# Attention and expert layer on one core: one layer norm a sequence ahead, a regrouped value product, and the differences to the maximum on GpSimd

## What is computed

```python
x = x + layernorm(attn(layernorm(x)))     # x: (16, 512, 128)
x = x + layernorm(ffn(layernorm(x)))
# attn: scores = einsum(Qh, Kh) + einsum(Qh, rel_k_table[clip(k - q, -2, 2) + 2]);  scores /= sqrt(8)
#       p = softmax(where(causal, scores, -1e9))
#       out = einsum(p, Vh) + einsum(p, rel_v_table[idx]);  return out @ W_o + b_o
# ffn:  shared silu(x @ sw1) * (x @ sw3) @ sw2, plus the two best of 8 gelu experts by sigmoid gates
```

## Time and profile before

| | us |
|---|---|
| median of 3 runs | 1033.69 (1032.93 to 1034.54) |
| profiled execution, its own time | 1030.79 |
| its span, first to last instruction | 1029.1 |
| attention, up to the last exponential | about 722 |
| a step with all four stages | about 41.5 |

### The profile page before, as it was taken

How to read it: one execution, slowest core, us unless ns; L and a number is a source line. 1 busy time by engine, 2 the same in 40 slices (tenths; PEclk the granted TensorE clock), 3 DMA queues, 4 the chain that set the end, 5 groups by cost and what they waited for, 6 DMA issues and landing times. The chain is left out here.

```text
span 1029.1 us, 25739 instructions
## 1 busy us (share of the span) xinstructions
PE 898.8 (87%) x8935; PEld 526.4 (51%) x8935; DVE 817.6 (79%) x1948; ACT 680.5 (66%) x1315; POOL 728.0 (71%) x946
## 2 busy tenths in 40 slices
PE   2888988999899988998999898887679999999995
PEld 0443444544445444444444444433357777777773
...
DMA packets 58828, 70.88 MB, mean 69 GB/s; under 512 B 8944, under 2 KB 34416, under 8 KB 58720
## 3 DMA queue, kind: packets, MB, share of 16 engines
...
q10 hardware_dynamic: 2288, 0.42, 0.2%
...
## 5 line engine op out<-in xcount | busy, mean ns | idle before, releaser
L1137 DVE TENSOR_REDUCE mx<-ps_s 128x1 f32<-128x512 f32 (+2 forms) x640 | 410.2, 682 | 75.2 <-PE ps_s L1549 74.2
L809 ACT ACTIVATE prob<-ps_e 128x512 f32<-128x512 f32 x640 | 352.0, 608 | 110.3 <-PE ps_e L1506 110.2
L651 POOL TENSOR_SCALAR_AFFINE_SELECT prob<-prob 128x516 f32<-128x516 f32 (+1 forms) x320 | 176.6, 576 | 150.2 <-ACT prob L809 150.1
L1530 PE MATMUL ps_s<-ks,qs 31*128 31x512 f16 (+3 forms) x1024 | 196.5, 324 | 32.2 <-DVE mx L1137 27.0
L1572 PE MATMUL ps_av<-prob,vp 128*32 128x512 f32 (+3 forms) x2048 | 202.5, 495 | 4.3 <-POOL prob L651 4.2
L731 POOL TENSOR_TENSOR hidden_low<-hidden,hidden_high 128x512 fp32r<-128x512 f32 x144 | 191.0, 1354 | 12.0 <-ACT hidden_high L998 10.7
L1506 PE MATMUL ps_e<-qs,ks 32*128 32x512 f16 (+3 forms) x1024 | 167.9, 316 | 6.2 <-ACT prob L809 2.0
L1530 PEld LDWEIGHTS ps_s<-ks,qs 31*128 31x128 f16 x1024 | 54.9, 94 | 167.6 <-issue 89.4
L1549 PE MATMUL ps_s<-masked_at,below 32*128 32x64 bf16 (+3 forms) x2560 | 135.0, 192 | 0.0
L998 ACT CAST hidden_high<-hidden 128x512 fp32r<-128x512 f32 x160 | 98.0, 613 | 30.7 <-DVE hidden L1450 27.5
L1549 PEld LDWEIGHTS ps_s<-masked_at,below 32*128 32x128 bf16 x2560 | 105.6, 98 | 20.0 <-issue 4.1
...
## 6 DMA issues: line engine op xcount, KB each, us to landing
gate_rows<-gates_dram SPq DMA_DIRECT2D x128, 256.0 KB, 3.7
...
```

What stands on the lines that cost most here:

```text
L651: pool.affine_select(out=v, in_=v, compare_op=ALU.is_ge, fill=0.0, base=-2, pattern=cols, channel_multiplier=-1).then_inc(S["p_masked"], 1)
L809: act.activation(prob[g % 2][:, u, b, :], ps_e[bank][:, :], ACT.Exp, scale=SCALE).then_inc(S["e_done"], 1)
L1137: dve.tensor_reduce(out, src, AX.X, ALU.max).then_inc(s_free[bank], 1)
L1530: pe.matmul(scores[:, at:at + P * (qt + 1)], qs[par][rows, pr, P * qt:P * qt + P], ks[par][rows, pr, 0:P * (qt + 1)], start=(n == 0), stop ...
```

## The change

Four things are changed at once, and the places of the side work on every engine with them.

1. **First norm one sequence ahead.** Norm1 of sequence t0+1 is made in step t0 (DVE's statistics and POOL's `normalise`), so that xT moves from round 6 to round 0. q moves from round 9 to 3 and k from 10 to 5. `xnT` has two buffers, since xT now writes the next sequence's before v0, moved from round 5 to 8, has read the one before. Sequence 2 is loaded by itself.
2. **Output projection in round 9** instead of 11; oT stays in 7. s_tok moves from 7 to 10.
3. **Value banks shared by two groups.** `vp` puts an odd group's columns 16 further than an even group's, and both groups add into one bank. So ACT copies, PE transposes and DVE reads two results (av0, av1) per sequence instead of four, each twice as wide; the values are copied on ACT in two halves.
4. **Differences on POOL.** The two DVE instructions for d in each `max_half` become one POOL instruction.

```diff
+AT = {"xT": 0, "e_sums": 1, "q": 3, "m1": 4, "k": 5, "av1": 6, "oT": 7, "v0": 8, "oproj": 9, "s_tok": 10,
+      "m0": 15, "av0": 17, "xn2": 18, "logits": 19}
...
-        vp = [sb(f"vp{i}", [P, NT, H, 32]) for i in range(2)]
+        vp = [sb(f"vp{i}", [P, NT * NGRP, 4, 2 * WIDE]) for i in range(2)]
...
+            def differences(st, s, half):
+
+                pool.wait_ge(S["m16_ready"], st.at(2 * s + half + 1, 2))
+                hs = slice(half * 8, half * 8 + 8)
+                pool.tensor_tensor(d01[:, :, :, hs], s_tok[:, :, :, hs],
+                                   m16[:, :, hs].unsqueeze(1).to_broadcast([P, 2, NT, 8]),
+                                   ALU.subtract).then_inc(S["d_ready"], 1)
...
                 if st.B:
+                    differences(st, st.b, 1)
                     near_half(st, st.b, 1)
-                masks(0, 3)
-                if st.F:
-                    normalise(st, st.f, xn[:, :, :], tiles(xr[:, st.seq(st.f), :]), mv1, var1, rs1,
-                              "stats1").then_inc(S["xn_ready"], 1)
-                masks(3, 10)
+                masks(0, 5)
                 if st.F:
                     split(st)
+                    if st.f + 1 < NSEQ:
+                        norm1(st.f + 1)
                 if st.t0 == 0:
                     masked_columns()
...
-                act.copy(vp[st.a % 2][:, :, :, 0:D].rearrange("p t h d -> p (t h) d"),
-                         ps_s[bank][:, :].rearrange("p (c d) -> p c d", d=D)).then_inc(S["v_ready"], 1)
+                of = ps_s[bank][:, :].rearrange("p (c j d) -> p c j d", j=4, d=D)
+                for q in range(2):
+                    last = act.copy(vp[st.a % 2][:, q::2, :, WIDE * q:WIDE * q + D], of[:, q::2])
+                last.then_inc(S["v_ready"], 1)
...
-            def av_out(st, s, g):
-
-                act.wait_ge(S["av_full"], st.at(NGRP * s + g + 1, NGRP))
-                act.copy(av_s[g % 2][:, :], ps_av[:, :]).then_inc(S["av_copied"], 1)
+            def av_out(st, s, part):
+
+                act.wait_ge(S["av_full"], st.at(NGRP * s + 2 * part + 2, NGRP))
+                act.copy(av_s[part][:, :], ps_av[:, :]).then_inc(S["av_copied"], 1)
...
+                need(dve, S["d_ready"], st.at(2 * st.a, 2))
...
-                for k in range(2):
-                    last = dve.scalar_tensor_tensor(d01[:, k, :, hs], m16[:, :, hs], -1.0, s_tok[:, k, :, hs],
-                                                    ALU.mult, ALU.add)
...
-                own.mark(dve.tensor_tensor(den[:, :, hs], v[:, :, :, D], p_near[par][:, :, 4 * g:4 * g + 4], ALU.add))
-                cols = slice(4 * g * D, 4 * g * D + 4 * D)
-                dve.tensor_tensor(num[:, :, hs, :], v[:, :, :, 0:D], near[par][:, :, cols].rearrange(
-                    "p t (j d) -> p t j d", d=D), ALU.add).then_inc(S["misc_free"], 1)
-                if g % 2 == 0:
-                    return
+                own.mark(dve.tensor_tensor(den[:, :, :, :], v[:, :, :, :, D], p_near[par][:, :, both].rearrange(
+                    "p t (q j) -> p q t j", q=2), ALU.add))
+                dve.tensor_tensor(num[:, :, :, :, :], v[:, :, :, :, 0:D], near[par][:, :, cols].rearrange(
+                    "p t (q j d) -> p q t j d", q=2, d=D), ALU.add).then_inc(S["misc_free"], 1)
...
+                after = st.t0 + 1 if 0 < st.t0 < NSEQ - 1 else None
...
-                if kt == 0:
-
-                    need(pe, S["av_copied"], st.at(NGRP * s + g, NGRP))
+                if kt == 0 and g % 2 == 0:
+
+                    need(pe, S["av_copied"], st.at(NPART * s + g // 2, NPART))
...
-                    last = pe.matmul(ps_av[32 * j:32 * j + 32, P * kt:SEQ], vp[par][:, kt, 4 * g + j, :],
+                    last = pe.matmul(ps_av[32 * j:32 * j + 32, P * kt:SEQ], vp[par][:, NGRP * kt + g, j, :],
                                      prob[g % 2][:, u, j % 2, at:at + w],
-                                     start=(kt == 0), stop=(kt == NT - 1))
+                                     start=(kt == 0 and g % 2 == 0), stop=(kt == NT - 1 and g % 2 == 1))
```

More of the change, by code:

```diff
@@ L208, in end @@
     def end(self):
-        if LOOP0 <= self.st.t0 < NSEQ and self.per_step != self.n - self.first:
+        if LOOP0 <= self.st.t0 < NSEQ - 1 and self.per_step != self.n - self.first:
             raise AssertionError((self.n - self.first, self.per_step))
@@ L322, in block_kernel @@
         av_s = [sb(f"av_s{i}", [P, SEQ]) for i in range(2)]
-        den = sb("den", [P, NT, 8])
-        rden = sb("rden", [P, NT, 8])
-        num = sb("num", [P, NT, 8, D])
+        den = sb("den", [P, 2, NT, 4])
+        rden = sb("rden", [P, 2, NT, 4])
+        num = sb("num", [P, 2, NT, 4, D])
         o_tok = sb("o_tok", [P, NT, P])
@@ L404, in block_kernel @@
         S = {n: sem(n) for n in names}
-        x_loaded = [S["x_loaded0"], S["x_loaded1"], S["x_loaded2"]]
+        x_loaded = [S[f"x_loaded{i}"] for i in range(4)]
         stacks = [[S[f"stacks{par}{half}"] for half in range(2)] for par in range(2)]
@@ L714, in step @@
                     selectors()
-                masks(12, 15)
+                masks(10, 14)
+                if st.A:
+                    differences(st, st.a, 0)
+                masks(14, 15)
                 if st.t0 == NSEQ + 2:
@@ L816, in xT_out @@
                 act.wait_ge(S["e_full"], n + 1)
-                act.copy(xnT[:, 1:1 + SEQ], ps_e[bank][:, :]).then_inc(S["e_done"], 1)
+                act.copy(xnT[st.f % 2][:, 1:1 + SEQ], ps_e[bank][:, :]).then_inc(S["e_done"], 1)
             def q_out(st):
@@ L1191, in av_tok_out @@
                 own.settle()
-                own.mark(dve.reciprocal(rden[:, :, :], den[:, :, :]))
+                own.mark(dve.reciprocal(rden[:, :, :, :], den[:, :, :, :]))
                 own.settle()
-                dve.wait_ge(S["misc_free"], st.misc(f"av{g}") + 1)
-                both = slice(4 * (g - 1) * D, 4 * (g + 1) * D)
-                dve.tensor_tensor(o_tok[:, :, both].rearrange("p t (j d) -> p t j d", d=D), num[:, :, :, :],
-                                  rden[:, :, :].unsqueeze(3).to_broadcast([P, NT, 8, D]),
+                dve.wait_ge(S["misc_free"], st.misc(f"av{part}") + 1)
@@ L1199, in av_tok_out @@
+                dve.tensor_tensor(o_tok[:, :, cols].rearrange("p t (q j d) -> p q t j d", q=2, d=D), num[:, :, :, :, :],
+                                  rden[:, :, :, :].unsqueeze(4).to_broadcast([P, 2, NT, 4, D]),
                                   ALU.mult).then_inc(S["o_ready"], 1)
@@ L1330, in step @@
                     gates_second(0, EARLY)
[L1331 removed]
+                maxima(13, 16)
                 if st.A:
[L1333 to L1334 removed]
+                    values_out(st)
+                maxima(16, 18)
                 if st.C:
```

195 lines of the change are left out of this document (94 added, 101 removed).

## The result

The changed kernel takes 1056.63 us in the median (1055.06 to 1068.95, 4 runs) against 1033.62: a ratio of 1.025, 95% interval 1.017 to 1.033. It is slower by 23 us where 1025 was forecast, 9 faster; that it is slower is beyond doubt, that it is so by over 2% is not. The profiled execution took 1058.02, its span is 1056.3, 27 above the profiled execution before.

A forecast was written before the change was run, and what follows sets the result against it. PE and its waits bound rounds 17 to 7 (-0.45), DVE rounds 8 to 16 (-0.2); with gaps and clock -0.6 a step, -8 over 13 steps, -8.7 with the ends: 1025, forecast 1016 to 1031 (0.42), whole range 1000 to 1046.

The forecast's parts named there:

- the term for q and k in rounds 8 to 16: Front of DVE's stretch: q and k, 2.24 us of PE, kept DVE short of score units; their leaving gains 2.2 a step.
- Rounds 17 to 7: Stretch over the turn of the step, paced by PE and what it waits for: forecast -0.45 us a step.
- out: v0, 1.16: Rounds 17 to 7: moving v0 to round 8 takes 1.16 us of PE work out of this stretch.
- Rounds 8 to 16: Stretch in which DVE sets the pace, with PE behind the s ring: forecast -0.2 us a step.
- PE pays for that once more: Projection, one round after v0: it needs the bank v_near empties; DVE being slower, the wait costs PE, not the end.
- ACT: Four copies between its sixth and tenth exponential, 1.7 us net; mostly covered by idle time, so +0.4 a step.
- Differences: d of the second half on POOL, 0.35 us, makes exponential p<-d about 1 us later: +0.4 a step, between 0 and 1.0.
- The clock: PE's lower 1.2 GHz level, which comes behind waits: its cost falls from 1.4 to 1.0 us a step.
- A: Rival, chance 0.24: ACT's copies and v0's bank outlast the gains, waits bring the low clock, +0.9 a step: 1044.
- D: Rival, chance 0.04: POOL's SBUF reads hold DVE back, o_tok's median over 700 ns, 1.9 us a step: 1050.
- C: Rival, chance 0.12: no change; DVE's work and waits set the step, its savings go into idling at v0: 1034.
- B: Rival, chance 0.18: without the waits for xr and xn the clock stays up, step 39.0: 1001.

The follow-up runs named there:

- e9: The changed kernel with q back in round 9 and k in round 10, their copies where they were before: 1018.5 us.
- h6: The e9 kernel with five idle products of a constant on PE ahead of round 3, without q's copies: 1023.1 us.
- e6: The changed kernel with v0 in round 9 and the output projection in round 11: 1037.5 us.
- e4: The changed kernel with eight idle products of a constant on PE ahead of the output projection in each step: 1039.7 us.
- h3: The changed kernel with k alone back in round 10, q left in round 3: 1065.6 us.
- h1: The e9 kernel with the differences to the maximum (d) back on DVE: 1019.2 us.

## Why the prediction was wrong

The step that failed first is the term for q and k in rounds 8 to 16, forecast as a gain of 2.2 a step: there they had cost nothing, and without q there PE stands before v0's bank and loses the clock. With q alone back in round 9 (h5) the kernel takes 1019.6 instead of 1056.6. The terms one by one:

**What bounds the kernel: wrong in its half.** "From round 17 to round 7 PE sets the pace" was read off a trace in which PE waits for xn in that stretch. Without that wait DVE is nearly always busy in rounds 2 to 6, too (idle 0.4 in e9). PE work placed there has no cover: 1.2 us of it in round 3 cost 0.65 a step (h6).

**Rounds 17 to 7, forecast -0.45 a step.** Measured: 23.6 against 23.1, so +0.5. The wait for xn did go, 1.3. The step that failed here is "out: v0, 1.16". v0 stands ahead of round 8, at the end of the same stretch, and left nothing; e6, which moves it on to round 9, has rounds 0 to 7 1.2 shorter. q and k cost what was said, 2.24.

**Rounds 8 to 16, forecast -0.2.** Measured: 20.5 against 18.3, so +2.2. The wait for v0 was sized right (1.8), in part by luck: the product ahead of v0 is not one of 1.07 in round 8 but that of round 7, 1.28. Two steps failed. "PE pays for that once more ... this wait costs PE and not the end": it was 1.7 us of stand, right before the low clock, and e4 shows 17 to 20 us in it. And "q and k, 2.24 of PE, ... are gone: I take -2.2": this was the largest term and had the wrong sign. In rounds 9 and 10 they were free and kept PE at work: rounds 8 to 10 take 6.5 us with both of them (e9) and with q alone (h5). q's place is worth 37 us (h5 against the changed kernel) or 47 (e9 against h3). That the trace shows no wait there was read as room to gain, when it was the cover that hid them.

**ACT**, 0.4 with bounds 0 to 1.7: the size is not parted from the clock, 9 to 15 us in all. **Differences**: 0.31 us on POOL (0.35 forecast), p<-d waits 9.3 us in ten times, 0.9 each (1 forecast), but of the +0.4 on the path nothing was found: with d on DVE the step is 0.3 longer (h1). **num**: 0.414 for one of two widths against 2 x 0.281, so 0.15 saved for each pair, and den 0.181 against 2 x 0.168, 0.16 saved: 0.3 together where the forecast had 0.56, which priced a double width like a single one.

**The clock**, forecast 1.0 instead of 1.4: it grew. Mean busy time of PE per step is 39.3 with less work than the 37.4 of the earlier trace rows, and the granted clock over twelve steps is 0.85 instead of 0.93. As there are only two levels, that is an estimated 13 us at 1.2 GHz in each step instead of 6.

**Start and end**: e_sums begins at 27.66 (27.2 forecast), below; the end gained 5, not 2, since the 5.0 of the earlier trace rows is gone whole.

```profile
27.66 1.06 PE L1634 MATMUL ps_misc<-e,head_sum 128*32 128x512 f32 x1 [0.29 <-POOL e L669]
```

**The rivals.** A named the place (v0's bank, ACT's copies, the clock) and 1044. Its threshold of 2.5 us for v_back was too high, as 1.8 was enough. It left out that q had been the cover, so even it was 12 us short, and the range to 1046 missed. D: its sign came, o_tok's median rose from 538 to 776, but not its cost: the median is 901 in e9, one of the fastest, and 458 in h1, equal in time with the differences back on DVE. Lengths from 424 to 1268 ns in e9 are what the rule of the Trainium skill (SBUF — State Buffer, "Who interferes with whom") would make of an instruction with two inputs in SBUF; that it is the cause no run shows. C and B are ruled out by the time.
